# A graph layer on one core: half of the first two blocks' degree sums by accumulating DMAs, layer-norm statistics by pairs, an own path for the first two tiles

## What is computed

```python
h = jnp.maximum(_layernorm(x, axis=-1), 0.0)
deg = jnp.sum(adj, axis=1, keepdims=True) + 1e-05
h_neigh = (adj / deg) @ h
out = x + relu(h_neigh @ W_neigh.T + b_neigh + h @ W_self.T + b_self)
```

## Time and profile before

| | us |
|---|---|
| median of three runs | 466.65 |
| the profiled execution | 467.36 |
| its span in the profile | 465.2 |
| TensorE busy | 424.9 (91%) |
| VectorE busy | 365.8 (79%) |
| ScalarE busy | 206.6 (44%) |
| GpSimd busy | 90.7 (19%) |

### The profile page before, as it was taken

The page is one execution under the profiler, slowest core; times in us unless marked ns, Lnnn a source line. Parts: engine busy times, 40 slices in busy tenths (PEclk is TensorE's granted clock), DMA queues, the critical chain, the costliest instruction groups (busy, mean ns, idle before and its releaser), DMA issues.

```text
span 465.2 us, 5515 instructions
## 1 busy us (share of the span) xinstructions
PE 424.9 (91%) x2048; PEld 353.3 (76%) x2048; DVE 365.8 (79%) x430; ACT 206.6 (44%) x265; POOL 90.7 (19%) x61
## 2 busy tenths in 40 slices
PE   1777788778979999999999999999999999999996
PEld 1555666556758889888888888888888888888885
DVE  3587779797997697776979699797979698887954
ACT  3355424652644554542644264444535264425411
POOL 1402331123000142330530040101320041003120
PEclk9998998989979999999999999999999999999999
DMA  8665354334464445455355537463655447454501
GB/s 310 253 243 173 128 173 143 110 137 161 151 213 137 135 137 180 133 184 181 132 186 181 180 137 222 148 201 108 216 168 183 160 135 250 157 180 136 181 1 45
DMA packets 21738, 76.64 MB, mean 165 GB/s; under 512 B 2384, under 2 KB 3664, under 8 KB 21328
## 3 DMA queue, kind: packets, MB, share of 16 engines
q1 hardware_dynamic: 21712, 76.29, 48.9%
HBM read 72.09 MB, written 4.19 MB: 164 GB/s over the span
## 4 chain that ended last, share of the span: by engine, by line
PE 70%; DVE 16%; POOL 6%; issue 4%; ACT 4%; DMA 1%; DVEq 0%; POOLq 0%
PE banks L460 19%; PE banks L461 19%; PE banks L462 19%; PE banks L486 10%; DVE total L353 6%; DVE adj_lo L341 5%; POOL rstd L193 3%; DVE stats L321 2%; ACT adj_hi L236 2%; POOL shift L191 2%; PE banks L477 2%; ACT h_row L239 1%; PE banks L510 1%; POOL rstd L190 1%; DVE mv L328 1%
## 5 line engine op out<-in xcount | busy, mean ns | idle before, releaser
L460 PE MATMUL banks<-adj_hi,h_hi 128*128 128x512 f32 x512 | 206.3, 403 | 36.1 <-DVE adj_lo L341 32.8
L341 DVE TENSOR_TENSOR adj_lo<-adj_raw,adj_hi 128x1024 fp32r<-128x1024 f32 x128 | 164.9, 1288 | 82.1 <-ACT adj_hi L236 81.9
L461 PE MATMUL banks<-adj_hi,h_lo 128*128 128x512 f32 x512 | 203.4, 397 | 0.0
L462 PE MATMUL banks<-adj_lo,h_hi 128*128 128x512 f32 x512 | 203.2, 397 | 0.0
L236 ACT ACTIVATE adj_hi<-adj_raw 128x1024 fp32r<-128x1024 f32 x128 | 135.1, 1056 | 150.0 <-PE banks L462 144.8
L353 DVE TENSOR_TENSOR total<-total,adj_raw 128x1024 f32<-128x1024 f32 x120 | 146.1, 1218 | 0.0
L460 PEld LDWEIGHTS banks<-adj_hi,h_hi 128*128 128x128 f32 x512 | 98.5, 192 | 62.4 <-issue 19.7
L462 PEld LDWEIGHTS banks<-adj_lo,h_hi 128*128 128x128 f32 x512 | 98.4, 192 | 21.5
L461 PEld LDWEIGHTS banks<-adj_hi,h_lo 128*128 128x128 f32 x512 | 98.2, 192 | 19.1
L208 POOL TENSOR_TENSOR x_sb<-x_sb,own 128x1024 f32<-128x1024 f32 x7 | 41.7, 5953 | 172.8 <-ACT own L290 172.8
L239 ACT ACTIVATE h_row<-x_sb,shift,rstd 128x256 f32<-128x256 f32 x64 | 33.9, 590 | 63.1 <-POOL shift L196 63.1
(11 more groups left out here) (40 smaller groups left out, 220.4 us busy)
## 6 DMA issues: line engine op xcount, KB each, us to landing
adj_raw<-adj_in SPq DMA_DIRECT2D x128, 512.0 KB, 3.3
rows_out<-x_sb SPq DMA_DIRECT2D x7, 512.0 KB, 4.9
x_sb<-x_in SPq DMA_DIRECT2D x3, 1024.0 KB, 5.5
x_sb<-x_in SPq DMA_DIRECT2D x2, 256.0 KB, 4.5
x_sb<-x_in SPq DMA_DIRECT2D x1, 512.0 KB, 8.0
rows_out<-x_sb SPq DMA_DIRECT2D x4, 128.0 KB, 1.7
w_raw<-w_neigh SPq DMA_DIRECT2D x1, 256.0 KB, 4.8
w_raw<-w_self SPq DMA_DIRECT2D x1, 256.0 KB, 5.1
```

The lines of the kernel that those rows point to most:

```text
L341: nc.vector.tensor_tensor(adj_lo[:, r, :, :], adj_raw[:, r, :, :], adj_hi[:, r, :, :].bitcast(F32), ALU.subtract).then_inc(s_lo, 1)
L460: nc.tensor.matmul(bank, h_hi[:, j, feats], adj_hi[:, r, a, :], start=first, stop=False)
L461: nc.tensor.matmul(bank, h_lo[:, j, feats], adj_hi[:, r, a, :], start=False, stop=False)
L462: done = nc.tensor.matmul(bank, h_hi[:, j, feats], adj_lo[:, r, a, :], start=False, stop=last)
```

## The change

- `by_dma` names 16 of the first 32 units (steps 1, 2, 5, 6, 9, 10 and so on). VectorE no longer adds them. Instead GpSimd starts a DMA for each that reads the unit again from HBM and, from the third on, adds it to a new tile `total_dma` (one half of it for either block) as it lands. Before it starts one it waits until TensorE has used unit 2n, and until the last DMA into the same half has landed. VectorE joins both totals before `join_sums` of blocks 0 and 1, which now stands two steps ahead of their `weigh_at`. `total` has three places in place of two.
- Statistics, norms and loads of x go by pairs of tiles, a pair's statistics and norm standing at step s for the pair used at step s + 4. SyncE loads 16 pairs in place of 6 parts.
- The first unit is loaded, split and multiplied in halves. The first two tiles of h are scaled on VectorE from mean and rstd (tensor_scalar), clipped and rounded on ScalarE. TensorE begins with nine matmuls on a zeroed tile whose result is not used.
- Last block: the degree sums stand before the last unit, the product @ W_neigh is done by feature halves over all four row tiles, and VectorE does four scalings, then the four last additions.

Cut to its core:

```diff
+WARM = 9
...
+    by_dma = [(q, u) for u in range(U) for q in range(2) if u % 2 != q]
+    by_vector = [order[s] not in by_dma for s in range(S)]
...
-                    sp.wait_ge(s_add, old + 1)
+                    if by_vector[old]:
+                        sp.wait_ge(s_add, vector_added[old])
...
-            load_x(0)
-            load_unit(0)
+            sp.dma_start(x_sb[:, 0, :], x[:, 0, :]).then_inc(s_x[0], 16)
+            sp.dma_start(adj_raw[:, 0, 0, :], adj[0, 0, :, 0, :]).then_inc(s_raw0, 16)
+            sp.dma_start(x_sb[:, 1, :], x[:, 1, :]).then_inc(s_x1, 16)
+            sp.dma_start(adj_raw[:, 0, 1, :], adj[0, 0, :, 1, :]).then_inc(s_raw[0], 16)
...
+            for s in range(RING, S):
                 load_unit(s)
+                if s % 2 == 0 and s // 2 + 2 < PAIRS:
+                    load_x(s // 2 + 2)
...
-                sp.wait_ge(s_last, 2 * b + 2)
+                sp.wait_ge(s_last, UI + b + 1)
...
+            def add_unit(n):
+
+                q, u = by_dma[n]
+                pool.wait_ge(s_used, 2 * n + 1)
+                if n >= 2:
+                    pool.wait_ge(s_dadd[q], 16 * (n // 2))
+                    pool.dma_start(total_dma[:, q, :, :], adj[q, u, :, :, :], accum_op=ALU.add).then_inc(s_dadd[q], 16)
+                else:
+                    pool.dma_start(total_dma[:, q, :, :], adj[q, u, :, :, :]).then_inc(s_dadd[q], 16)
...
-            norm(0)
+            first_norm(0)
+            first_norm(1)
+            first_shift()
...
+            norm(2, slice(2, 4), 3)
             for s in range(S):
-                if s >= 2 and s <= 26 and (s - 2) % 4 == 0:
-                    norm((s - 2) // 4 + 2)
+                if s % 2 == 0 and s // 2 + 2 < PAIRS:
+                    p = s // 2 + 2
+                    norm(p + 1, slice(2 * p, 2 * p + 2), p + 2)
+                if s % 2 == 1 and s // 2 < len(by_dma):
+                    add_unit(s // 2)
...
+            first_half_unit(0)
+            first_split(0)
+            first_split(1)
+            first_half_unit(1)
+            make_h(1)
+            for s in range(1, S):
...
+                if q < 2:
+                    dve.wait_ge(s_dadd[q], 16 * (len(by_dma) // 2))
+                    nc.vector.tensor_tensor(total[:, q % 3, :, :], total[:, q % 3, :, :], total_dma[:, q, :, :], ALU.add) \
...
+            nc.vector.memset(p_hi[:, 0, :].bitcast(F32), 0.0).then_inc(s_warm, 1)
...
+            statistics((0,), 1)
+            dve.wait_ge(s_x1, 16)
+            statistics((1,), 2)
+            first_scaled(0)
+            first_scaled(1)
+            first_low(0)
+            first_half_unit(0)
+            first_low(1)
+            first_half_unit(1)
+            pair_statistics(1)
             add_unit(0)
-            dve.wait_ge(s_x[1], 16)
-            statistics(1)
-            means(1)
             split_unit(1)
...
+                if s % 2 == 0 and s // 2 + 2 < PAIRS:
+                    pair_statistics(s // 2 + 2)
+                if by_vector[s]:
+                    add_unit(s)
...
+            degrees(Q - 1)
             product_low(Q - 1)
-            degrees(Q - 1)
...
+            def first_unit():
+
+                for a in range(UJ):
+                    for stage, (m, high) in enumerate(((h_hi, adj_hi), (h_lo, adj_hi), (h_hi, adj_lo))):
...
+                        for k in range(KC):
+                            done = nc.tensor.matmul(banks[:, MAIN[0][k], :], m[:, a, k * P:(k + 1) * P], high[:, 0, a, :],
+                                                    start=(a == 0 and stage == 0), stop=False)
...
+            def weigh_last():
+
+                pe.wait_ge(s_owned, Q)
+                for k in range(KC):
+                    pe.wait_ge(s_plo, 2 * (Q - 1) + k + 1)
+                    for t in range(UI):
+                        cols = slice(t * P, (t + 1) * P)
+                        for n, (m, w) in enumerate(((p_hi, w_hi), (p_hi, w_lo), (p_lo, w_hi))):
+                            last = nc.tensor.matmul(banks[:, TAIL[t], 0:F], m[:, k, cols], w[:, k, 0, :],
+                                                    start=(k == 0 and n == 0), stop=(k == KC - 1 and n == 2))
+                        if k == KC - 1:
+                            last.then_inc(s_weighed, 1)
+
+            pe.wait_ge(s_warm, 1)
+            for _ in range(WARM):
+                nc.tensor.matmul(banks[:, SMALL[0], :], p_hi[:, 0, 0:P], p_hi[:, 0, :], start=True, stop=True)
+            first_unit()
+            for s in range(1, S):
+                if s == S - 1:
+                    sum_degrees(Q - 1)
                 add_unit(s)
```

More of the change, by code:

```diff
@@ L63, in gnn_layer @@
         own = sb("own", [P, UI, F])
-        total = sb("total", [P, 2, UJ, R])
+        total = sb("total", [P, 3, UJ, R])
+        total_dma = sb("total_dma", [P, 2, UJ, R])
         sums = sb("sums", [P, R])
@@ L101, in gnn_layer @@
         s_add = sem("unit_added")
+        s_dadd = [sem(f"unit_added_by_dma{q}") for q in range(2)]
         s_used = sem("adj_unit_used")
@@ L184, in _, with norm @@
         def _(pool):
-            def norm(g):
-                a, b = groups[g]
-                cols, n = slice(a, b), b - a
+            def norm(g, cols, need):
+                n = cols.stop - cols.start
                 mean, var = mv[:, cols, 0], mv[:, cols, 1]
-                pool.wait_ge(s_mv, g + 1)
+                pool.wait_ge(s_mv, need)
                 nc.gpsimd.tensor_tensor(rstd[:, cols], var, consts[:, 0, 0:n], ALU.add).then_inc(s_rstd, 1)
@@ L247, in make_h, with first_split, first_half_unit @@
                 normalise(2 * p + 1, h_row[:, p % 2, 1, :]).then_inc(s_h, 1)
+            def first_split(a):
+                act.wait_ge(s_y, a + 1)
+                nc.scalar.activation(h_hi[:, a, :], h_row[:, 0, a, :], ACT.Relu).then_inc(s_hhi0, 1)
+            def first_half_unit(a):
+                act.wait_ge(*((s_raw0, 16) if a == 0 else (s_raw[0], 16)))
+                nc.scalar.activation(adj_hi[:, 0, a, :], adj_raw[:, 0, a, :], ACT.Copy).then_inc(s_hi0 if a == 0 else s_hi, 1)
             def split_h(p):
-                act.wait_ge(s_h, p + 1)
+                act.wait_ge(s_h, p)
                 nc.scalar.activation(h_hi[:, 2 * p:2 * p + 2, :], h_row[:, p % 2, :, :], ACT.Copy).then_inc(s_hhi, 1)
@@ L290, in relu @@
                 nc.scalar.activation(own[:, :, :], own[:, :, :], ACT.Relu).then_inc(s_relu, 1)
-            make_h(0)
-            split_h(0)
-            for s in range(S):
+            first_half_unit(0)
[4 more added lines that the diff above has]
+            for s in range(1, S):
                 split_unit(s)
@@ L317, in _, with statistics, pair_statistics, first_scaled @@
         def _(dve):
-            def statistics(g):
-                a, b = groups[g]
-                for t in range(a, b):
+            def statistics(tiles, need):
+                for t in tiles:
                     last = nc.vector.bn_stats(stats[:, t, :], x_sb[:, t, :])
                 last.then_inc(s_stats, 1)
-            def means(g):
-                a, b = groups[g]
-                dve.wait_ge(s_stats, g + 1)
-                for t in range(a, b):
+                dve.wait_ge(s_stats, need)
+                for t in tiles:
                     last = nc.vector.bn_aggr(mv[:, t, :], stats[:, t, :])
                 last.then_inc(s_mv, 1)
+            def pair_statistics(p):
+                dve.wait_ge(s_x[p], 16)
+                statistics((2 * p, 2 * p + 1), p + 2)
+            def first_scaled(t):
+                dve.wait_ge(s_rstd, 2 * t + 2)
+                nc.vector.tensor_scalar(h_row[:, 0, t, :], x_sb[:, t, :], mv[:, t, 0:1], rstd[:, t:t + 1],
+                                        ALU.subtract, ALU.mult).then_inc(s_y, 1)
+            def first_low(t):
+                dve.wait_ge(s_hhi0, t + 1)
+                nc.vector.scalar_tensor_tensor(out=h_lo[:, t, :], in0=h_row[:, 0, t, :], scalar=0.0,
+                                               in1=h_hi[:, t, :].bitcast(F32), op0=ALU.max, op1=ALU.subtract) \
+                  .then_inc(s_hlo0 if t == 0 else s_hlo, 1)
+            def first_half_unit(a):
+                dve.wait_ge(*((s_hi0, 1) if a == 0 else (s_hi, 1)))
+                nc.vector.tensor_tensor(adj_lo[:, 0, a, :], adj_raw[:, 0, a, :], adj_hi[:, 0, a, :].bitcast(F32),
+                                        ALU.subtract).then_inc(s_lo0 if a == 0 else s_lo, 1)
             def split_h(p):
-                dve.wait_ge(s_hhi, p + 1)
+                dve.wait_ge(s_hhi, p)
                 nc.vector.tensor_tensor(h_lo[:, 2 * p:2 * p + 2, :], h_row[:, p % 2, :, :],
@@ L435, in _ @@
             for t in range(UI):
-                row = (Q - 1) * UI + t
                 dve.wait_ge(s_weighed, 2 * (Q - 1) + t + 1)
```

119 lines of the change are left out of this document (62 added, 57 removed).

## The result

The changed kernel takes 449.87 us (median of 4 runs, 448.25 to 450.46) against 467.06 for the kernel before on the same chip: a ratio of 0.9653, 95% interval 0.962 to 0.9686 (the two medians divide to 0.963, inside the interval). The forecast was 435, the range 428 to 450: faster, but with 17 us gained of the 32 forecast. The profiled execution, at 448.25 us the fastest of the four, has a span of 446.2 us, 19.0 less than before.

The account below looks back on a forecast made before the run. GpSimd's norm loop was to bound units 5 to 31 at 2.84 us, TensorE the rest. Unit 32's start 105.0 + steps 32 to 127 319.6 + tail 8.65 = 433.3 us span, + 2.16 around it, less 0.7: 435 us, range 428 to 450.

Parts of the forecast that it names:

- D: GpSimd's time to start one accumulating transfer between two norms, taken as 1.0 us.
- the loop of 11.35 us for four units: Steps 5 to 31: norm of 4.3 us, ScalarE and VectorE work up to the next statistics; 2.84 us a unit.
- GpSimd is the bound: Rival, first part: D of 2 us or norm of 5.5 gives 3.15 us a unit, 443 us; chance 0.22.
- That fits, if an added byte costs as a loaded one.: Queues in the first part: 1.84 MB for two units in 5.46 us, 336 GB/s against 403 in the trace.
- The rival of the queues: First part: an added byte costs as two, 5.9 us a pair, 438 and up to 445 us; chance 0.14.
- 76.7 + 1.6 = 78.3: From unit 5 to unit 32: 27 units at 2.84 us, plus 1.6 us for w_lo and b_sum.
- 322.6 - 3.0 = 319.6: Steps 32 to 127: the former time less 3.0 us for unit 32's wait for p_lo and half clock.
- ScalarE: four h rows and two p_hi; VectorE no longer late: Ahead of unit 32: p_lo(0) comes 2.5 us after unit 30, within unit 31's 2.73, so no wait.
- 8.65: Tail: 8.16 us before plus 0.5 (sums +0.79, products by halves -0.6, stores +0.3).
- Slower: Rival: same-half transfer waits hold GpSimd; additions decide from 11 us, 493 us total at 20; chance 0.03.
- Nothing moves: Rival: norm of 8.3 us keeps the loop at 15.33 us for four units, only the start gives, 460; chance 0.03.
- TensorE alone: Rival: norm near 1.3 to 3 us, so TensorE is the bound in the first part, 430 us; chance 0.08.

Follow-up runs that it names:

- e11: Only statistics, norms and x loads by pairs, two pairs ahead, put on the kernel before: 450.08 us, 0.9643.
- e3: The changed kernel with its accumulating transfers as plain copies (degrees of blocks 0 and 1 lack those units): 443.74 us, 0.9518.
- e14: e9 with plain copies for the accumulating transfers (degrees of blocks 0 and 1 lack those units): 436.35 us, 0.9364.
- e12: e5 without the nine warming matmuls: 445.84 us, 0.9556.
- e1: The changed kernel with all additions on VectorE, no added transfers and no joins: 447.25 us, 0.9594.
- e6: The changed kernel with the split of block 0's product (p_hi, p_lo) at step 32, not 33: 450.08 us, 0.9657.
- e8: e1 with the split of block 0's product at step 32: 445.65 us, 0.9564.
- e5: The changed kernel with block 1's totals joined at VectorE's step 38, not 41: 444.15 us, 0.9536.
- e9: The changed kernel with e5's and e6's moves, and block 0's join and sums at step 36, TensorE's sums two steps later: 440.75 us, 0.9451.
- e10: Only the last block's edits put on the kernel before: 467.3 us, 1.0012.

## Why the prediction was half right

**What bounds the kernel, and the pair statistics.** Right, and it is nearly the whole gain. The chain statistics, GpSimd, make_h was the link; by pairs, two ahead, it goes (e11 alone gives 0.9643). What is left in e11 is VectorE, with 39.57 us busy of 40. The transfers then exchange VectorE's bound for the queues', which by itself is no gain.

**GpSimd's norm and D.** The sizes were right: 3.9 us against 4.3 beside a busy VectorE, 0.9 against 1.0. The conclusion was wrong: the loop of 11.35 us for four units took the norm as always slow, while it is slow only when VectorE is busy, and takes 2.8 us on average. e3 and e14 have the norms, the starts and a full TensorE. The rival "GpSimd is the bound" falls with it.

**The accumulating byte.** This is the step that failed in the first part: "That fits, if an added byte costs as a loaded one." It costs about 1.8 times as much packet time, the queues are full up to 100 us, and raw units come late. The rival of the queues was the right mechanism for the first part; it forecast 2.93 us a unit (its own sum) and 438 to 445 us. Units 5 to 31 took 80.3 us (27.4 to 107.7), where the forecast had 76.7 + 1.6 = 78.3. With plain copies (e14) they took 75.1 (28.86 to 103.92, a wait of 0.35 us ahead of unit 32 left out). So the addition cost 5.2 us here, and the forecast missed by 2.0 only because the GpSimd loop and the weights, for which it had counted more than they cost, hid the other 3.2.

**Start.** Unit 0 at 6.39 (forecast 5.4), unit 1 at 14.94 (14.2), unit 5 at about 27.4 (26.7): 0.7 late by unit 5. The warming matmuls show no gain that e12 can tell, as the text said they would save little.

**Steps 32 to 127.** "322.6 - 3.0 = 319.6", the wait for p_lo gone. It stayed, 2.88 us, with half the clock behind it. "ScalarE: four h rows and two p_hi; VectorE no longer late" is the step that failed: p_lo(0) was done 5.5 us after unit 30 and not 2.5. It left out VectorE's own row, in which p_lo stands behind the work of units 32 and 33, adj_lo, copy, adj_lo and an addition, without a gap from 105.25 us on. That the last raw units land late (two waits for adj_raw stand right ahead of ScalarE's h rows) comes on top but isn't the cause: e1, whose queues are not full, waits 2.82 us as well, and moving the split by one step brings the wait to 0.47 (e6) and 0.55 us (e8).

**The joins.** The other step that failed in the second part was one never made: the two joins, 1.22 us each, were part of the change and had no price. Block 1's stands on VectorE in a stretch in which four scalings, the sums and GpSimd's x_sb addition stand too. That the joins decide is shown by e5 (moving one by three steps takes the rest from 335.6 to 331.1 us) and e9, which moved block 0's with its sums. The join costs more than itself because it lets GpSimd's addition start before adj_lo: 1.25 us of its own and 2.2 of adj_lo, as the two traces show (3.43 us in the changed kernel, 1.22 in e5). Before, adj_lo took 2.23 us at that addition, but behind ht_lo and not ahead of it. No run moved GpSimd's addition by itself.

**Tail.** 8.0 us from the last unit and 0.8 for the sums ahead of it, against 8.65: right, and its edits alone change nothing that e10 can tell.

**The other rivals.** Slower: one transfer lands in 8.4 us, under the 11 from which that case decides. Nothing moves: refuted by T32. TensorE alone: not so in the changed kernel, but TensorE is full from 20 to 60 us in e3 and e14, once the bytes are plain.

**The sum again.** The profiled span of 446.2 us lies 12.9 above the 433.3 of the sum: 0.7 for the start, 2.0 for units 5 to 31, 2.9 for the wait for p_lo and 7.3 behind it. Of the 7.3, 1.6 are the half clock in unit 32 (against e9), 3.2 the wait for ht_lo and 1.5 the half clock behind that; about 1 us is not placed.

By experiments the miss of 0.9653 - 0.9364 = 0.029, 13.5 us, comes apart in two measured steps: 9.4 us (0.9653 to 0.9451) for where joins, sums and block 0's product stand, and 4.1 us (0.9451 to 0.9364) for the additions in the queues. The larger part lay in the places of small work on VectorE, the smaller in the price of an added byte. With both taken away the kernel takes 436.35 against the forecast's 435. That closeness is in part luck: in e14 unit 5 starts 2.2 us later than forecast, units 5 to 31 take 3.2 less, and the rest takes 1.8 more (0.93 of it a wait for ht_lo). The measured time lies at the upper edge of the range, 449.87 of 450, and by the ratio, 0.9653 of the 466.65 from which the forecast started, at 450.5, just outside; the range was not made for misses in one direction.

## What to carry to other kernels

Price every instruction that an edit adds, the joins of a split sum too, and at the place where it stands: between work that an engine waits for, 1.2 us on VectorE cost 4.5 (e5), elsewhere nothing that shows. A transfer that adds took nearly twice the queue time of one that copies, so count its bytes twice, and against a rate that the trace holds for long: 2 us at 403 GB/s were not it. And when a stall goes, look for the next thing that the same late engine owes: e6 removed one wait and got it back 13 us later; only when all of them had moved (e9) did the time come through.

## What the runs showed of the chip

- A 512 KB transfer with addition lands in 8.4 us (median) with full queues; a plain one of the same size to the same place in 7.2 (e3) and 7.0 (e14), while the packet time differs by a factor of 1.8.
- A wait of TensorE of about 3 us was followed by half the clock for some 2.5 us or more (2.88 us at unit 32, granted clock 0.57 up to 113.10; 3.80 us in e6 at 121.72, 0.56 up to 125), and waits of 0.65 and 1.10 us in e9 were not (1.00), nor was one of 2.51 us in the kernel before (at 117.07, 1.00).
- VectorE's adj_lo, which reads two SBUF operands, and GpSimd's x_sb addition exclude each other: adj_lo begins at 143.66, GpSimd's addition ends at 146.00, and adj_lo ends 1.09 later, at 147.09; in e5 adj_lo starts first and takes 1.22, and GpSimd's addition takes 6.24 in place of 2.95. The Trainium skill (SBUF — State Buffer, Who interferes with whom) says that a VectorE instruction with two SBUF inputs contends with a GpSimd instruction that reads SBUF, and the trace agrees.
- Starting an accumulating transfer took GpSimd 0.86 to 0.93 us in each of 14 cases, a plain one of the same shape 0.53 to 0.60 (e3), beside VectorE's work too.
